# Last layer of a four-layer kernel: router and row numbers in another place of the order, maxima split at other points, expert tiles in slots 4 to 13

## The chip, the cores and the metric

The kernel is one program on one core of one Trainium2 chip. The metric is the device time of a launch in microseconds (us). Five engines run their own instruction streams side by side and meet at semaphores: TensorE (PE in the profile), VectorE (DVE), ScalarE (ACT), GpSimd (POOL) and SyncE (SP), which here only issues transfers. PEld is TensorE loading weights.

## The reference, cut to what matters

Four layers in a row work on `x` of 4 x 1024 x 128. Only the last one is touched. It normalizes `x` and adds a causal attention of 16 heads (8 wide) and a mixture of 8 experts of which each row takes the best two:

```python
    qkv = (x @ W_qkv + b_qkv).reshape(b, s, h, 3 * hd)
    logits = jnp.einsum('bshd,bkhd->bhsk', q, k) / np.sqrt(hd)
    logits = jnp.where(mask[None, None, :, :], -jnp.inf, logits)
    attn = jax.nn.softmax(logits, axis=-1)
    out = jnp.einsum('bhsk,bkhd->bshd', attn, v).reshape(b, s, d)
    return out @ W_out + b_out
...
    router_logits = x_flat @ router_w.T
    router_probs = jax.nn.softmax(router_logits, axis=-1)
    top_k_probs, top_k_idx = jax.lax.top_k(router_probs, TOP_K)
    top_k_probs = top_k_probs / (top_k_probs.sum(axis=-1, keepdims=True) + 1e-08)
    cw = (jax.nn.one_hot(top_k_idx, E, dtype=x.dtype) * top_k_probs[..., None]).sum(axis=1)
    for e in range(E):
        h = new_gelu(x_flat @ w1[e].T + b1[e])
        out_e = h @ w2[e].T + b2[e]
        output = output + cw[:, e:e + 1] * out_e
...
    x = x + _L3_attn_ref(xn, ...) + _L3_ffn_ref(xn, ...)
```

## The kernel before

The last layer is one stage, `attn3_stage`, in which attention and experts are interleaved by hand. Attention is cut into 16 combinations `c` of a batch and a group of four heads. The stage runs over 19 **slots** of 48 **places**; tables of places (`SCORES_AT`, `SUMS_AT` and so on) say at which place of a slot every engine does which piece. All engines walk the same loops, so the tables set the order on each.

Slot `s` works on three things at a time:

- Scores of combination `s` (slots 0 to 15): PE `score` (L2794, with the causal constants at L2799), 20 units, each read by DVE `largest` (L3221), which keeps row maxima. At the slot's end DVE reduces them (L3331).
- Maxima of `s - 1`: PE turns them (`turn_max`, key "Z", L2807), DVE copies them (`turned_max`, L3228), POOL splits them into three bfloat16 parts (`split_max`, five instructions, L3365 to L3369), SP writes them beside the queries (`maxima`, L2680, six DMAs).
- The transposed scores of `s - 2` (`scoreT`, L2822): PE can't begin them before these DMAs have landed. ACT takes the exponential (L3013), POOL zeroes the masked half of the diagonal blocks (`causal`, L3375; for combinations 0, 14 and 15 PE does this at L2829), PE multiplies with the values (`sums`, L2848).

The experts: DVE `route` (L3164 to L3177) makes from the router's product the two best experts of each row and their shares; PE `count` (L2773, L2774) sums the one-hot rows; DVE `slots` (L3184 to L3206) turns the counts into a slot number for each of 2 x 4096 rows, sorted by expert. POOL scatters the rows by 64 indirect DMAs of 128 rows (L3389) to `expert_rows`. They are processed as 39 tiles of 256 rows, each with its own expert's weights: SP `load_tile` (five DMAs, L2691 to L2697; it waits until all scatters have landed), PE turns the rows (L2865), multiplies up (L2875) and down (L2885), ACT does the gelu between (L3023), DVE copies, SP stores. At the end POOL gathers the results back by 64 indirect DMAs (L3380) and DVE adds them, scaled, to `x` (`combine`, 16 instructions a batch, L3285). Slots 1, 5 and 9 also project the next batch (`project`), slots 6, 10, 14 and the end add the attention's output to `x`.

Three tables matter here. `FIRST_SLOT, LAST_SLOT` spread the 39 tiles evenly over slots 3 to 13, which gives 3, 4, 3, 4, 3, 4, 3, 4, 3, 4, 4. `SPREAD` and `SCATTER` say after which score unit (slots 0 and 1) and which group of four places (slot 2) POOL issues scatters. `SPLIT_AT` says before which group POOL does the split: 8 up to slot 15, 2 in slot 16. POOL runs its stream in order, so a scatter ahead of a split holds it up. Only two PSUM bank pairs serve the scores, the maxima, the row transposes and the down products; they are handed out in turn (`s_at`, `take_s`), and each taker waits for the reader of the last but one.

Of the kernel before, what the change touches and what calls it, by code (L numbers as in the profile page):

```python
# [23 lines left out]
B, S, D = 4, 1024, 128  # L24
# [3 lines left out]
NCH = TOK // CH  # L28
# [2256 lines left out]
def layer2(k, L):  # L2285
    with ExitStack() as ctx:
# [10 lines left out]
NI = B * NG  # L2297
# [25 lines left out]
PARTS_AT = (4, 13, 16, 19, 22, 40, 42)  # L2323
MAX_AT, SPLIT_AT = (2, 20), (8, 2)
SUMS_AT = (7, 13, 16, 19, 22, 29, 30, 34, 40, 47, 47), \
# [5 lines left out]
OUT_AT = (42, 41), (32, 37)  # L2331
FIRST_SLOT, LAST_SLOT = 3, 13
PROJECT = {1: 1, 5: 2, 9: 3}
PER_SLOT = {s: range((s - FIRST_SLOT) * NTILE // (LAST_SLOT + 1 - FIRST_SLOT),
                     (s + 1 - FIRST_SLOT) * NTILE // (LAST_SLOT + 1 - FIRST_SLOT))
            for s in range(FIRST_SLOT, LAST_SLOT + 1)}
GATHER = {14: (0,), 15: (1,), 16: (2,), 17: (3,)}
SPREAD = ((0, 0, 0, 1, 1, 1, 1, 1, 1, 1, 1, 1, 1, 1, 2, 2, 2, 2, 2, 2), (1, 1, 1, 1, 1, 1, 1, 1, 1, 1, 1, 1, 1, 1, 1, 1, 2, 2, 2, 2))
SCATTER = (3, 3, 3, 3, 3, 2, 0, 0, 0, 0, 0, 0)
ON_PE = (0, NI - 2, NI - 1)  # L2340
# [78 lines left out]


def max_turned(s, place):
    return 0 <= s - 1 < NI and place == MAX_AT[s >= NI]
# [27 lines left out]
def ring_tables():  # L2450
# [7 lines left out]
    def add(table, key):  # L2458
        table[key] = len(table)

    def project(b, part):
        if part < 2:
            for t in range(2):
                add(t_at, ("P", b, part, t))
        elif part == 2:
            add(s_at, ("V", b))
# [5 lines left out]
    for i in range(2, NCH):  # L2472
        add(t_at, ("N", i))
    project(0, 2)
    add(s_at, ("G",))
    for s in range(SLOTS + 1):
        b = s - 2
        for place in range(PLACES):
# [18 lines left out]
            for bb, u in by_batch(s, place, OUT_AT):  # L2497
                add(s_at, ("Y", bb, u))
            if s == 0 and place == 3:
                add(s_at, ("C",))  # L2500
            for bb, part in projected(s, place):
# [4 lines left out]
def attn3_stage(k, R):  # L2506
# [15 lines left out]
    with ExitStack() as ctx:  # L2522
# [99 lines left out]
        with nc.Block() as block:  # L2622
# [121 lines left out]
            def _(pe):  # L2744
# [24 lines left out]
                def count():  # L2769
                    bank = take_s("C")  # L2770
                    when(pe, VR, "cw1")
                    all_hot = hot.rearrange("p r t e -> p (r t e)")
                    pe.matmul(k.ps[:, bank, :], k.triu[:], all_hot, start=True, stop=True)  # L2773
                    pe.matmul(k.ps[:, bank + 1, :], k.ones[:], all_hot, start=True, stop=True).then_inc(s_done, 1)  # L2774
# [153 lines left out]
                for i in range(3, NCH):  # L2928
                    turn_normed(i)
                    route(i - 1)  # L2930
                project(0, 2)
                route(NCH - 1)
                pe.wait_ge(ready, 9)
                pe.wait_ge(o_zero, 1)
                for s in range(SLOTS + 1):
                    b = s - 2
                    for place in range(PLACES):
# [19 lines left out]
                        for x, u in by_batch(s, place, OUT_AT):  # L2957
                            out_project(x, u)
                        if s == 0 and place == 3:
                            count()  # L2960
                        for x, part in projected(s, place):
# [121 lines left out]
            def _(dve):  # L3083
# [212 lines left out]
                rest_low(0)  # L3296
                normalize(7)
                values(0)
                route()
                dve.wait_ge(mx_zero, 1)  # L3300
                for s in range(SLOTS + 1):
                    first = s
                    for place in range(PLACES):
# [10 lines left out]
                        for x, u in by_batch(s, place, MERGE_AT):  # L3314
                            out_turned(x, u)
                        for x, u in by_batch(s, place, OUT_AT):
                            residual(x, u)
                        if s == 0 and place == 3:
                            slots()
                        for x, part in projected(s, place):  # L3320
# [12 lines left out]
                    for n in GATHER.get(s - 1, ()):  # L3333
                        combine(n)

            @block.gpsimd
            def _(pool):
# [56 lines left out]
                for s in range(SLOTS):  # L3394
# [6 lines left out]
                    if s >= 2:  # L3401
                        pool.wait_ge(parts, min(s - 1, NI))
                        for g in range(GROUPS):
                            if g == SPLIT_AT[s >= NI] and s - 1 < NI:
                                split_max(s - 1)
                                pool.wait_ge(parts, s)
# [148 lines left out]
```

## Time and profile before

| what | value |
|---|---|
| median of 3 runs | 2204.67 us (2203.06 to 2205.88) |
| the profiled execution | 2206.71 us, of which the trace's span is 2204.9 us |
| PE busy in the span | 1872.5 us (85%) |
| DVE, ACT, POOL busy | 1787.8, 1380.7, 1296.8 us |
| the last layer's slots in the span | from about 1509 us to the end |

A page of the profile gives each engine's busy time; an answer of the trace gives instructions in order of time, with the idle time before them and who ended it, or the busy time of each engine in stretches. The stretches used below are the slots as PE runs them. "x16" behind an instruction is a run of 16 alike, merged; the time then is that of the run.

### The profile page before, as it was taken

How to read it: one execution, taken by the hardware profiler on the slowest of the kernel's cores; microseconds unless marked ns; L12 is line 12 of the kernel's file. 1: busy time of each engine (PE TensorE's matmuls, PEld its weight loads, DVE VectorE, ACT ScalarE, POOL GpSimd, SP SyncE). 2: the span in 40 equal slices, each digit the busy share in tenths (PEclk: the TensorE clock that was granted, in tenths of full speed). 3: DMA queues.
4: the chain of work that ended last, by engine and by line, in shares of the span. 5: the costliest groups of instructions: out<-in, count | busy, mean ns of one | idle time of the engine just before them, and what ended most of it. 6: DMA issues, size and time to landing. Idle time of an engine off the chain costs nothing. (4 is left out here: it accounts for less than half of the span.)

```text
span 2204.9 us, 32675 instructions
## 1 busy us (share of the span) xinstructions
PE 1872.5 (85%) x10276; PEld 996.0 (45%) x10276; DVE 1787.8 (81%) x2181; ACT 1380.7 (63%) x2604; POOL 1296.8 (59%) x954
## 2 busy tenths in 40 slices
PE   5898989888989897777988499985759999999986
PEld 5333333333333333333565288863325455455532
DVE  6699999999999999977878899987847667667783
ACT  3676666666666666456335577761347777777766
POOL 4799999999998999932226255552741111111276
PEclk7999999999999999899998699995679999999998
DMA  3355444555444455540102000002333333333212
GB/s 79 112 160 149 151 156 157 154 156 166 143 151 149 153 155 155 159 134 0 31 12 81 1 0 0 0 19 77 85 98 94 103 112 94 103 113 94 76 38 75
DMA packets 156309, 217.53 MB, mean 99 GB/s; under 512 B 31722, under 2 KB 68602, under 8 KB 155546
## 3 DMA queue, kind: packets, MB, share of 16 engines
q1 hardware_dynamic: 152074, 207.41, 31.1%
q0 software_dynamic: 4096, 8.40, 1.5%
q8 instruction: 72, 1.18, 0.2%
q14 instruction: 67, 0.55, 0.1%
HBM read 196.59 MB, written 23.86 MB: 100 GB/s over the span
## 5 line engine op out<-in xcount | busy, mean ns | idle before, releaser
L1035 POOL TENSOR_TENSOR m_dBx<-m_du,m_rowB 128x1024 f32<-128x1024 f32 x256 | 605.0, 2391 | 4.4 <-DMA m_rowB<-bc_rows 4.2
L758 PE MATMUL ps<-m_hC,ident 128*128 128x512 f32 x1024 | 513.3, 648 | 99.1 <-DVE m_hC L1117 99.0
L3221 DVE TENSOR_REDUCE a_mx<-ps 128x2 f32<-128x1024 f32 (+2 forms) x320 | 345.0, 1114 | 113.5 <-PE ps L2794 55.6
L934 ACT ACTIVATE ps<-m_delta,m_A 128x512 f32<-128x512 f32 x512 | 332.7, 682 | 143.4 <-DVE m_hC L1117 112.7
L3013 ACT ACTIVATE a_pT<-ps 128x512 f32<-128x512 f32 (+2 forms) x640 | 317.9, 561 | 155.4 <-PE ps L2822 137.1
L758 PEld LDWEIGHTS ps<-m_hC,ident 128*128 128x128 f32 x1024 | 203.7, 207 | 391.9 <-issue 232.0
L3375 POOL TENSOR_SCALAR_AFFINE_SELECT a_pT<-a_pT 128x512 f32<-128x512 f32 x104 | 66.1, 637 | 390.1 <-ACT a_pT L3013 388.6
L1117 DVE TENSOR_TENSOR m_hC<-ps,m_rowC 128x1024 f32<-128x1024 f32 x176 | 215.4, 1224 | 16.7 <-issue 1.3
L1108 DVE TENSOR_TENSOR_SCAN ps<-ps,m_dBx 128x1024 f32<-128x1024 f32 x88 | 201.1, 2285 | 33.2 <-ACT ps L934 21.2
L1045 POOL TENSOR_TENSOR m_hC<-m_h,m_rowC 128x1024 f32<-128x1024 f32 x80 | 194.5, 2432 | 46.0 <-DVE m_h L1108 45.8
L1108 DVE TENSOR_TENSOR_SCAN ps<-ps,m_carry,m_dBx 128x1024 f32<-128x1024 f32 x88 | 206.3, 2345 | 5.5 <-ACT m_dBx L959 4.6
L2848 PE MATMUL ps<-a_pT,l_v 128*9 128x512 f32 (+3 forms) x1536 | 161.1, 500 | 2.3 <-POOL a_pT L3375 1.9
L2794 PE MATMUL ps<-a_k,a_q 48*128 48x512 bf16 (+3 forms) x768 | 132.8, 352 | 28.4 <-DVE a_mx L3221 18.1
L2822 PE MATMUL ps<-a_q,a_k 51*128 51x512 bf16 (+3 forms) x768 | 123.0, 339 | 31.9 <-ACT a_pT L3013 16.9
L713 PE MATMUL ps<-pad,e_conv_w 128*128 128x512 f32 x256 | 116.6, 599 | 1.2 <-DVE m_diag L1069 1.2
L2822 PEld LDWEIGHTS ps<-a_q,a_k 51*128 51x128 bf16 x768 | 36.3, 95 | 133.4 <-ACT a_pT L3013 92.6
L1108 DVE TENSOR_TENSOR_SCAN m_h<-ps,m_carry,m_dBx 128x1024 f32<-128x1024 f32 x40 | 93.6, 2341 | 0.0
L1108 DVE TENSOR_TENSOR_SCAN m_h<-ps,m_dBx 128x1024 f32<-128x1024 f32 x40 | 91.3, 2282 | 1.5 <-POOL m_dBx L1035 0.6
L3389 POOL DMA_INDIRECT expert_rows<-l_xn,l_slot x64 | 61.7, 964 | 48.1 <-DVE a_mx L3221 31.9
L2146 POOL TENSOR_TENSOR c_xw<-c_x,l_wb 128x256 f32<-128x256 f32 x32 | 19.6, 613 | 102.4 <-ACT c_x L2193 102.4
L2794 PEld LDWEIGHTS ps<-a_k,a_q 48*128 48x128 bf16 x768 | 39.0, 97 | 90.2 <-DVE a_mx L3221 59.1
L2885 PE MATMUL ps<-a_w,a_h 128*128 128x128 f32 x624 | 78.4, 280 | 0.0
(410 smaller groups left out, 3601.5 us busy)
## 6 DMA issues: line engine op xcount, KB each, us to landing
m_rowB<-bc_rows SPq DMA_DIRECT2D x256, 256.0 KB, 4.0
m_rowC<-bc_rows SPq DMA_DIRECT2D x256, 256.0 KB, 3.5
a_w<-in_L3f_w1T SPq DMA_DIRECT2D x39, 256.0 KB, 2.6
a_w<-in_L3f_w2T SPq DMA_DIRECT2D x39, 256.0 KB, 3.8
expert_rows<-in_zero_rows SPq DMA_DIRECT2D x39, 128.0 KB, 2.6
a_xs<-expert_rows SPq DMA_DIRECT2D x39, 128.0 KB, 2.3
expert_out<-a_y SPq DMA_DIRECT2D x39, 128.0 KB, 3.6
qk_parts<-a_part SPq DMA_DIRECT2D x18, 256.0 KB
```

The source lines that it names most:

```text
L713: mm = pe.matmul(o, wk[:, d, tap, c * P:c * P + P], pad[:, b * ROW + shift:b * ROW + shift + CH], start=tap == 0, stop=tap == CONV - 1)
L758: mm = pe.matmul(ps[:, bankY + c, :], k.ident[:], hC[:, n % NBUF, c, :], start=False, stop=n % NS == NS - 1)
L934: act.activation(decays(n)[:, c, :], delta[:, i % 2, c, chunk(i, x)], ACT.Exp, scale=An[:, ITEMS[i][0], c, s:s + 1]).then_inc(decayed, 1)
L1035: pool.tensor_tensor(dBx[:, n % NBUF], du[:, i % 2, :, chunk(i, x)], rowB[:, n % 4, :].unsqueeze(1).to_broadcast([P, HALF, CH]), ALU.mult) ...
L1045: pool.tensor_tensor(hC[:, n % NBUF], states(n), rowC[:, n % 4, :].unsqueeze(1).to_broadcast([P, HALF, CH]), ALU.mult).then_inc(hc_pool, 1)
L1108: dve.tensor_tensor_scan(time(states(n)), time(decays(n)), time(dBx[:, n % NBUF]), carry[:, s, f:f + 1] if x else 0.0, ALU.mult, ALU.add). ...
L1117: dve.tensor_tensor(hC[:, n % NBUF], states(n), rowC[:, n % 4, :].unsqueeze(1).to_broadcast([P, HALF, CH]), ALU.mult).then_inc(hc_dve, 1)
L2794: mm = pe.matmul(k.ps[:, bank + r, j * w:j * w + w], qs[u][rows, e, t * P:t * P + P], ks[u][rows, e, x:x + w], start=True, stop=not diag, ...
L2822: mm = pe.matmul(k.ps[:, tbank(n + r), j * w:j * w + w], ks[u][rows, e, kt * P:kt * P + P], qs[u][rows, e, q0:q0 + w], start=True, stop=no ...
L2848: mm = pe.matmul(k.ps[32 * hd:32 * hd + HD + 1, bankO, CH - w:CH], R["v"][:, c, kt, hd, :], pT[:, g % 3, hd, 0:w], start=kt == 0, stop=kt ...
L3013: act.activation(dst, src, ACT.Exp).then_inc(t_read, 1)
L3221: dve.tensor_reduce(mx[:, c % 2, :, es[0]:es[0] + len(es), t, x // CH], src, AX_X, ALU.max)\
```

## The change

- The router's last product is issued ahead of the values' product on PE (`project(0, 2)`), and DVE's `route` ahead of `values(0)`. `count` and `slots` leave place 3 of slot 0 and stand ahead of slot 0. `count` waits for the last step of the top-two search ("r_hot2") and no more for the shares.
- The scatters are dealt out anew (the sum is 64 in both): 20 and 30 in slots 0 and 1 instead of 23 and 24, 14 instead of 17 in slot 2. The split of slot 2 stands at group 0, ahead of that slot's scatters.
- The first tile slot is 4 instead of 3: the 39 tiles now lie as 3, then nine times 4.
- At the end: combination 15's maxima are turned at place 2 of slot 16 instead of 20, and split at group 0 instead of 2; the gathers of batches 2 and 3 are both issued in slot 16; the last `combine` stands between the last `out_turned` and the last `residual`, instead of behind it.

```diff
-MAX_AT, SPLIT_AT = (2, 20), (8, 2)
+MAX_AT, SPLIT_AT = (2, 2), (8, 0)
-FIRST_SLOT, LAST_SLOT = 3, 13
+FIRST_SLOT, LAST_SLOT = 4, 13
-GATHER = {14: (0,), 15: (1,), 16: (2,), 17: (3,)}
+GATHER = {14: (0,), 15: (1,), 16: (2, 3)}
...
+def split_at(s):
+    return MAX_AT[0] // 4 if s == 2 else SPLIT_AT[s >= NI]
...
-                    when(pe, VR, "cw1")
+                    when(pe, VR, top2_names("r")[-1])
...
+                route(NCH - 1)
                 project(0, 2)
-                route(NCH - 1)
+                count()
...
-                        if s == 0 and place == 3:
-                            count()
...
+                route()
                 values(0)
-                route()
+                slots()
...
                             out_turned(x, u)
+                            if (x, u) == (B - 1, 1):
+                                combine(x)
...
-                        if s == 0 and place == 3:
-                            slots()
...
                     for n in GATHER.get(s - 1, ()):
-                        combine(n)
+                        if n < B - 1:
+                            combine(n)
...
-                            if g == SPLIT_AT[s >= NI] and s - 1 < NI:
+                            if g == split_at(s) and s - 1 < NI:
```

What this does on PE at the layer's front. Before (L2764 router, L2756 values, L2794 and L2799 first scores, L2773 and L2774 `count`):

```order
L2764 MATMUL ps<-l_router,xnT 128x8 x4
L2756 MATMUL ps<-l_wqkv,xnT 128x128 x8
L2764 MATMUL ps<-l_router,xnT 128x8 x4
L2794 MATMUL ps<-a_k,a_q 128x128 x2
L2799 MATMUL ps<-a_consts_bf 128x128 x4
L2794 MATMUL ps<-a_k,a_q 128x128 x2
L2799 MATMUL ps<-a_consts_bf 128x128 x4
L2773 MATMUL ps<-a_h,triu 128x512
L2774 MATMUL ps<-a_h,ones 128x512
```

And now (the same lines stand five further down in the file):

```order
L2769 MATMUL ps<-l_router,xnT 128x8 x8
L2761 MATMUL ps<-l_wqkv,xnT 128x128 x8
L2778 MATMUL ps<-a_h,triu 128x512
L2779 MATMUL ps<-a_h,ones 128x512
L2799 MATMUL ps<-a_k,a_q 128x128 x2
L2804 MATMUL ps<-a_consts_bf 128x128 x4
```

The router's last four products moved ahead of the values, and the first score unit behind `count`.

On POOL, from the first scatter to the first masks, before (each run of L3365 to L3369 is a split):

```order
L3389 DMA expert_rows<-l_xn,l_slot 9984x128 x24
L3365 CAST a_m_parts<-a_mT 32x128
L3366 TENSOR_TENSOR a_mr<-a_mT,a_m_parts 32x128
L3367 CAST a_m_parts<-a_mr 32x128
L3368 TENSOR_TENSOR a_mr<-a_mr,a_m_parts 32x128
L3369 CAST a_m_parts<-a_mr 32x128
L3389 DMA expert_rows<-l_xn,l_slot 9984x128 x40
L3365 CAST a_m_parts<-a_mT 32x128
```

And now, where L3371 to L3375 is the split and L3395 the scatter:

```order
L3395 DMA expert_rows<-l_xn,l_slot 9984x128 x21
L3371 CAST a_m_parts<-a_mT 32x128
L3372 TENSOR_TENSOR a_mr<-a_mT,a_m_parts 32x128
L3373 CAST a_m_parts<-a_mr 32x128
L3374 TENSOR_TENSOR a_mr<-a_mr,a_m_parts 32x128
L3375 CAST a_m_parts<-a_mr 32x128
L3395 DMA expert_rows<-l_xn,l_slot 9984x128 x29
L3371 CAST a_m_parts<-a_mT 32x128
```

The second split has 50 scatters ahead of it instead of 64; the other 14 stand behind it, ahead of the first mask.

On DVE at the program's end (L3262 `out_turned`, L3270 `residual`, L3285 `combine`), before:

```order
L3241 TENSOR_TENSOR a_att<-ps,a_rs 128x4x32
L3262 COPY a_aT<-ps 128x512
L3270 TENSOR_TENSOR x_tm<-x_tm,ps 128x512
L3285 SCALAR_TENSOR_TENSOR x_tm<-a_h,l_cwr,x_tm 128x128 x16
```

And now, the same three at L3266, L3289 and L3274:

```order
L3245 TENSOR_TENSOR a_att<-ps,a_rs 128x4x32
L3266 COPY a_aT<-ps 128x512
L3289 SCALAR_TENSOR_TENSOR x_tm<-a_h,l_cwr,x_tm 128x128 x16
L3274 TENSOR_TENSOR x_tm<-x_tm,ps 128x512
```

The last `combine` moved ahead of the last `residual`.

## Rows read from the trace of the kernel before

**Rows 1.** Slots 3, 11, 12, 13, 15: length; busy PE, PEld, DVE, ACT, POOL; clock, DMA, GB/s

```profile
1627.00:1674.50 47.50, 38.43 (x343) 19.79 (x343) 25.18 (x31) 28.13 (x56) 6.53 (x13) 0.82 0.42 123
...
1968.70:2004.50 35.80, 35.30 (x351) 18.75 (x343) 25.69 (x33) 27.92 (x56) 6.67 (x14) 1.00 0.33 93
2004.50:2043.90 39.40, 39.00 (x377) 22.28 (x369) 26.59 (x35) 29.58 (x60) 6.76 (x14) 1.00 0.34 96
2043.90:2083.20 39.30, 38.89 (x377) 22.28 (x369) 26.49 (x35) 29.58 (x60) 6.66 (x14) 1.00 0.22 65
...
2112.70:2141.20 28.50, 24.02 (x270) 8.40 (x267) 24.88 (x32) 20.73 (x42) 21.47 (x28) 1.00 0.15 38
```

**Rows 2.** DVE in order of time: start us, us, instruction, count [idle before <-releaser]

```profile
1507.69 1.68 DVE L3150 TENSOR_TENSOR l_v<-ps,l_bias_v 128x128 f32<-128x128 f32 x8 [10.66 <-PE ps L2756]
1509.28 0.41 DVE L3164 COPY a_h<-ps 128x256 f32<-128x256 f32 x1
...
1517.15 0.42 DVE L1160 TENSOR_TENSOR a_h<-l_iota,a_h 128x256 f32<-128x256 f32 x1
...
1522.79 0.69 DVE L3184 COPY a_h<-ps 128x512 f32<-128x512 f32 x1 [3.21 <-PE ps L2774]
...
1531.56 20.48 DVE L3221 TENSOR_REDUCE a_mx<-ps 128x4 f32<-128x1024 f32 x19
```

**Rows 3.** PE in order of time, at the layer's front

```profile
1504.25 3.40 PE L2756 MATMUL ps<-l_wqkv,xnT 128*128 128x128 f32 x16
1507.49 0.96 PE L2764 MATMUL ps<-l_router,xnT 128*128 128x8 f32 x8
...
1519.00 2.04 PE L2773 MATMUL ps<-a_h,triu 128*128 128x512 f32 x2 [8.97 <-DVE l_cwr L3177]
```

**Rows 4.** POOL in order of time, slots 0 to 2

```profile
1535.48 1.23 POOL L3389 DMA_INDIRECT expert_rows<-l_xn,l_slot  x1 [29.03 <-DVE a_mx L3221]
...
1566.15 1.45 POOL L3366 TENSOR_TENSOR a_mr<-a_mT,a_m_parts 32x128 f32<-32x128 f32 x1
...
1619.18 0.95 POOL L3389 DMA_INDIRECT expert_rows<-l_xn,l_slot  x1 [0.30 <-issue]
...
1621.84 0.28 POOL L3369 CAST a_m_parts<-a_mr 32x128 bf16<-32x128 f32 x1
```

**Rows 5.** SP's issues in order of time, between slots 2 and 3

```profile
1622.14 3.73 SPq L2680 DMA_DIRECT2D a_q<-a_m_parts  x6
1627.03 0.41 SPq L2691 DMA_DIRECT2D a_xs<-expert_rows  x1
```

**Rows 6.** PE at the start of slot 3, in order of time

```profile
1627.08 0.61 PE L2822 MATMUL ps<-a_q,a_k 51*128 51x512 bf16 x2 [12.70 <-DMA a_q<-a_m_parts]
...
1632.91 0.66 PE L2865 MATMUL ps<-ident,a_xs 128*128 128x128 f32 x2 [4.04 <-DMA a_w<-in_L3f_w2T]
...
1639.46 0.66 PE L2865 MATMUL ps<-ident,a_xs 128*128 128x128 f32 x2 [2.53 <-DMA a_w<-in_L3f_w2T]
```

**Rows 7.** Line L2865, PE's idle time ahead of it: releaser, us, times

```profile
  DMA a_w<-in_L3f_w2T: 8.4, 3
```

**Rows 8.** DVE in order of time, slots 15 to 18

```profile
2112.96 0.22 DVE L3331 TENSOR_REDUCE a_m<-a_mx 128x32 f32<-128x64 f32 x1
...
2139.62 5.42 DVE L3285 SCALAR_TENSOR_TENSOR x_tm<-l_xn,l_cwr,x_tm 128x128 f32<-128x128 f32 x16
...
2196.90 4.29 DVE L3285 SCALAR_TENSOR_TENSOR x_tm<-a_h,l_cwr,x_tm 128x128 f32<-128x128 f32 x16 [4.88 <-DMA a_h<-expert_out,l_slot]
```

**Rows 9.** POOL in order of time, slots 16 to 18

```profile
2151.84 0.28 POOL L3365 CAST a_m_parts<-a_mT 32x128 bf16<-32x128 f32 x1 [4.33 <-issue]
...
2154.23 0.98 POOL L3380 DMA_INDIRECT a_h<-expert_out,l_slot  x1 [0.41 <-POOL a_m_parts L3369]
...
2161.96 2.59 POOL L3380 DMA_INDIRECT a_h<-expert_out,l_slot  x1 [0.30 <-ACT a_pT L3013]
...
2194.29 0.96 POOL L3380 DMA_INDIRECT a_h<-expert_out,l_slot  x1 [0.30 <-issue]
```

More of the change, by code:

```diff
@@ L2336 @@
             for s in range(FIRST_SLOT, LAST_SLOT + 1)}
-GATHER = {14: (0,), 15: (1,), 16: (2,), 17: (3,)}
-SPREAD = ((0, 0, 0, 1, 1, 1, 1, 1, 1, 1, 1, 1, 1, 1, 2, 2, 2, 2, 2, 2), (1, 1, 1, 1, 1, 1, 1, 1, 1, 1, 1, 1, 1, 1, 1, 1, 2, 2, 2, 2))
-SCATTER = (3, 3, 3, 3, 3, 2, 0, 0, 0, 0, 0, 0)
+GATHER = {14: (0,), 15: (1,), 16: (2, 3)}
+SPREAD = ((1,) * 20, (1, 2) * 10)
+SCATTER = (4, 4, 4, 2, 0, 0, 0, 0, 0, 0, 0, 0)
 ON_PE = (0, NI - 2, NI - 1)
@@ L2473, in ring_tables @@
         add(t_at, ("N", i))
+    add(s_at, ("G",))
     project(0, 2)
-    add(s_at, ("G",))
+    add(s_at, ("C",))
     for s in range(SLOTS + 1):
@@ L2498, in ring_tables @@
                 add(s_at, ("Y", bb, u))
-            if s == 0 and place == 3:
-                add(s_at, ("C",))
             for bb, part in projected(s, place):
@@ L3315, in _ @@
                             out_turned(x, u)
+                            if (x, u) == (B - 1, 1):
+                                combine(x)
                         for x, u in by_batch(s, place, OUT_AT):
                             residual(x, u)
-                        if s == 0 and place == 3:
-                            slots()
                         for x, part in projected(s, place):
```

## The prediction, made before the changed kernel was run

> **What bounds the kernel now.** I read the last layer first, since nothing else is touched, and there the busy time by stretch, one stretch a slot as PE runs it. In the middle of the layer PE is the bound: slot 11 with three tiles lasts 35.8 us, of which PE is busy 35.30, slots 12 and 13 with four tiles 39.4 and 39.3, of which 39.00 and 38.89, at the full clock [rows 1]. So there PE's work costs what it takes, and waits elsewhere cost nothing. Three places are not like that; the reader should look there for who is late.
>
> Ahead of slot 3 PE does nothing for 12.70 us and is then released by the DMA of the maxima [rows 6]. SP issued it from 1622.14 us on, right behind the split that ended at 1622.12, and that split began the moment the last scatter was done, at 1620.13 [rows 4, 5]. So the bound is POOL's queue of 64 scatters, begun at 1535.48, each 0.95 us of work and 0.30 of idle time, 1.26 together [rows 4].
>
> Slot 3 itself lasts 47.5 us, though it has three tiles like the slot of 35.8. PE waits three times for a tile's weights, 8.4 us in all, because the loads were issued only at 1627.03, behind maxima and scatters, and the granted clock is 0.82 of full [rows 1, 5 to 7].
>
> At the end DVE adds batch 3's results from 2196.90 on, after 4.88 us of waiting for the last gather. POOL issued that one at 2194.29: its gathers went on only at 2154.23, behind a split for which it had waited 4.33 us, since PE turns those maxima at place 20 [rows 8, 9].
>
> **The front, 4.5 us.** DVE's `route` starts at 1509.28; the top-two search ends at 1517.57, 8.29 into it, and the last share releases PE's `count` at 1519.00 [rows 2, 3]. `route` had waited for the router's last product, which stood behind the values' 3.4 us on PE [rows 3]. Now that product is done at 1504.25 + 0.9 = 1505.15, so `route` starts at about 1505.3, the search ends at 1513.6 and the shares at 1514.9. `count` starts at 1513.6 and takes what it took before, 1519.00 to 1522.75; so `slots` starts at 1517.4 instead of 1522.79. `values` (1.68) fits between, 1514.9 to 1516.6. `slots` takes 1531.56 - 1522.79 = 8.77 [rows 2] and ends at 1526.2. One score unit (0.69) that had been read ahead of it comes behind it now, with 0.2 for a bank pair that is free late: 1526.2 + 0.9 + 20.5 = 1547.6 against 1552.0 [rows 2], 4.5 us earlier. Slot 0 is DVE's to bound, slot 1 by and large too, so I carry the 4.5 on to slot 2. Bounds: 3.0, if the shift meets PE at its low clock in another way, and 5.4, the whole shift of `slots`.
>
> **POOL's wait, 12.7 us.** Scatters can start when the first score unit has been read, 1526.9, and 1 us after it, 1527.9. Then come 21 of them (26.5 us), a split, 29 more (36.6) and the second split. That one took 2.0, from 1620.13 to 1622.12; the first took longer, since one of its steps took 1.45 where the later ones take 0.4 [rows 4]; I give it 2 to 4. So the second is done at 1595.0 to 1597.0. SP takes 3.73 for the maxima, and PE had them 1.2 later [rows 5, 6]: 1600 to 1602. PE wants them 4.5 us earlier than the 1614.4 at which it ran dry, at 1609.9. The wait is gone with 8 us to spare. What is late next on POOL: 14 scatters (17.7 us) stand behind that split, to 1613 to 1615, and the first mask of slot 3 wants POOL at about 1613. I put 0 for it, since there are three buffers of exponentials, and 1 in the range.
>
> **Slot 3 without tiles, 20.5 us.** The nearest row is slot 15, no tiles and no projection: 28.5 us by the stretch, with masks between gathers on POOL, and 2139.62 - 2112.96 = 26.7 us from the end of one slot's maxima on DVE to the end of the next [rows 1, 8]. I take 27.0, since slot 3 has no gathers; bounds 26.5 and 30. 47.5 - 27.0 = 20.5 saved, of which 8.4 are waits for weights and most of the rest work that goes elsewhere.
>
> Will those waits come back at slot 4? SP issues the four loads behind `maxima(2)`. POOL splits these right after slot 3's fourth mask, since groups 4 to 7 make it wait for nothing: I put that 10 us into the slot and its end at 12 (an estimate from slot 15's order). Then 3.7 for the maxima, 1.2 to the first load, 5.9 from first load to first use, and (1639.46 - 1632.91) / 2 = 3.3 for each further tile [rows 5, 6]: 23, 26 and 29 us. The first three are wanted at 27, 29 and 29. So I put 0, and up to 8.4 in the range.
>
> **The tiles moved, -10.5 us.** Of 39 tiles three leave slot 3 and one slot 4; slots 5, 7, 9 and 11 take them. So three more lie in slots where PE is the bound. The fourth tile's price is 39.3 - 35.8 = 3.5 us; the mean of the first three, (35.8 - 27) / 3 = 2.9, is the lower bound [rows 1]. The upper one is 4.5, since slots 5 and 9 also project and I can't part their cost. 3 x 3.5 = 10.5.
>
> **The end, 3.5 us.** Combination 15's maxima are turned at place 2; DVE copies them once `combine(0)` is done, at 2139.62 + 5.42 = 2145.04 [rows 8]. The split runs 2145.5 to 2147.5, and 32 gathers follow from 2147.9, where 30 began at 2154.23. One at 2161.96 took 2.59 us, 1.63 more than its neighbours, and I count two such [rows 9]. The last is issued at 2147.9 + 31 x 1.26 + 2 x 1.63 = 2190.2, 4.0 earlier. It lands 2.6 later, as before, so the last `combine` (4.29) runs 2192.8 to 2197.1; the residual behind it ends at 2197.9. The last write was at 2196.90 + 4.29 = 2201.19 [rows 8]. That is 3.3, and one of the two stores that follow goes out earlier: 3.5. Bounds: 0, if the maxima's copy is late, and 5.
>
> Those held-up gathers, both in the midst of a `combine` on DVE: the row shows 2.59 where the last one shows 0.96 [rows 9]. The Trainium skill, "SBUF — State Buffer", section "Who interferes with whom", says that a VectorE instruction with two SBUF inputs contends with a GpSimd instruction that reads SBUF, and whichever comes second is blocked; by that rule, the trace agrees. If it did not hold here, the last gather would be issued 3.3 us earlier still and the end would give 6.8 instead of 3.5.
>
> **Sum.** 4.5 + 12.7 + 20.5 - 10.5 + 3.5 = 30.7 us less. Against the profiled execution, 2206.71 us (span 2204.9 and 1.8 around it), 2176.0. The median of the runs, 2204.67, stands 2.0 below the profiled one: 2174.0. All terms at their best give 5.4 + 12.7 + 21.0 - 8.7 + 5 = 35.4, which is 2169; all at their worst 3.0 + 11.7 + 17.5 - 13.5 + 0 - 8.4 = 10.3, which is 2194.
>
> **Rivals.** *The weights are late again.* The loads land in slot 4 as they did in slot 3, and PE waits up to 8.4 us. For it: the third tile is due just when it is wanted, by an estimate of POOL's place. Against: the first has 4 us. It gives 30.7 - 8.4 = 22.3 less, 2182. Chance 0.12.
>
> *POOL stays the bound.* If scatters are held up as the gather at 2161.96 was, by DVE's `slots`, by the subtractions of slot 1's projection or by reads in SBUF, the second split comes later. It decides from 8 us of delay on, that is from five such hold-ups; with ten, 16 us, PE waits 8 again and the change gives 22 less, 2183. Against: in the old order 64 scatters kept their pace beside the same maxima. Chance 0.07.
>
> *The wait moves to the masks.* The 14 scatters behind the second split hold up slot 3's first mask. At 1615 instead of 1613 it is nothing; with the hold-ups of the last rival, 5 to 8 us later, all of it is lost in slot 3: 23 to 26 less, 2179 to 2182. Then the change wouldn't do what it says. Chance 0.08.
>
> *Four tiles a slot cost more than PE's share.* In nine slots in a row SP has four loads and four stores ahead of the stacks of slot `s + 2`, and two bank pairs serve four tiles beside the scores. If that cost 3.4 us a slot on top, nine times, the 30.7 would be gone; beyond it the kernel is slower than before, 2207 with 3.7. Against it: slots 12 and 13 had four tiles one behind the other, at 39.4 and 39.3 with PE busy all but 0.4 [rows 1]. Chance 0.03.
>
> **How the numbers follow.** The rest, 0.70, is the forecast, 2174, with 2168 to 2180 as its own range. The next three rivals reach to 2183 or so, some of their cases beyond 2186. So 2168 to 2186 leaves out 0.15 to 0.2. Faster by over 0.2% (4.4 us, about what a measurement of this kernel can tell from no change) takes in all but the last rival and the worst sums: 0.96; within it 0.02; slower 0.02.
>
> **What would show it right or wrong.** In the changed kernel's trace: `slots` starting at 1517.4; the second split at about 1593 to 1595 behind 50 scatters, and PE not waiting for a maxima DMA at slot 3; a slot 3 of 27 us at the full clock; no wait of the first row transposes for weights; slots 7 and 11 at 39.3 us; in the last slot the last `combine` waiting for a gather that is issued 4 us sooner after slot 16's start than before. A slot 4 over 40 us, a gap at slot 3's first masks, or slots 5 and 9 longer by much more than 3.5 would make it wrong at that term.

## The result, and the profile after

The changed kernel takes 2173.18 us (median of 4 runs, 2171.57 to 2177.9); the kernel before 2205.28 in the same comparison. The ratio is 0.9864, with a 95% interval of 0.9843 to 0.9885: 1.4% faster. In a second set of runs it was 2173.24 us, ratio 0.9862 (0.9846 to 0.9879). 2174.0 had been forecast. The profiled execution took 2173.8 us, its span is 2172.0.

Runs of the same kernel differ by several us. Most of that lies ahead of the last layer, where nothing was changed, so I measure inside the layer, from anchors on DVE: the end of its last normalization (L3118 before, L3122 after) is the layer's start, and the start of the reduce that closes each combination's maxima (L3331, now L3336) ends a slot. Before, the layer took 707.87 us from its start to the span's end; now 677.06, which is 30.81 less, where 30.7 was forecast. All stretches below lie between these anchors, so "slot 3" is from slot 2's reduce to slot 3's.

| stretch | before | after | less | forecast |
|---|---|---|---|---|
| slots 0 to 2 | 117.46 | 112.90 | 4.56 | 4.5 |
| slot 3 | 60.42 | 28.79 | 31.63 | 33.2 (12.7 + 20.5) |
| slots 4 to 15 | 464.57 | 474.67 | -10.10 | -10.5 |
| behind slot 15 | 65.42 | 60.70 | 4.72 | 3.5 |

The busy time by stretch of the changed kernel, for slots 0, 3, 4, 5, 7 and behind slot 15. The columns are start and end, length, busy PE, PEld, DVE, ACT, POOL with counts, PE's granted clock, DMA share, GB/s:

```profile
1494.94:1546.19 51.25, 31.12 (x184) 18.97 (x184) 38.92 (x69) 3.90 (x7) 24.20 (x20) 0.57 0.28 90
...
1607.84:1636.63 28.79, 24.98 (x267) 8.94 (x265) 22.93 (x26) 20.77 (x42) 9.88 (x17) 0.94 0.40 119
1636.63:1672.46 35.83, 35.32 (x345) 18.76 (x343) 25.67 (x33) 27.92 (x56) 6.69 (x13) 1.00 0.33 97
1672.46:1720.43 47.97, 44.78 (x393) 25.50 (x389) 32.73 (x47) 37.50 (x69) 6.05 (x12) 1.00 0.31 88
...
1764.86:1804.15 39.29, 38.89 (x371) 22.28 (x369) 26.52 (x35) 29.58 (x60) 6.69 (x13) 1.00 0.33 92
...
2111.30:2172.00 60.70, 43.32 (x477) 16.95 (x477) 23.93 (x80) 39.38 (x85) 38.27 (x41) 0.89 0.28 74
```

And of the kernel before, slot 3, slot 5 and the end:

```profile
1614.49:1674.91 60.42, 38.84 (x345) 19.91 (x347) 25.77 (x33) 28.13 (x56) 12.81 (x23) 0.77 0.35 104
...
1714.24:1758.41 44.17, 41.11 (x367) 21.92 (x363) 31.99 (x44) 35.62 (x65) 6.05 (x12) 1.00 0.35 101
...
2139.48:2204.90 65.42, 45.08 (x477) 18.03 (x477) 24.03 (x80) 39.62 (x85) 39.20 (x41) 0.83 0.26 69
```

In slot 3 PE was idle for 60.42 - 38.84 = 21.6 us and is now idle for 3.8. The later slots have PE busy almost throughout, as the prediction read them from [rows 1].

**The front**, against [rows 2, 3]. DVE and PE of the kernel after, in order of time:

```profile
1504.06 0.42 DVE L3168 COPY a_h<-ps 128x256 f32<-128x256 f32 x1 [9.12 <-PE ps L2769]
...
1511.94 0.42 DVE L1160 TENSOR_TENSOR a_h<-l_iota,a_h 128x256 f32<-128x256 f32 x1
...
1516.30 0.69 DVE L3188 COPY a_h<-ps 128x512 f32<-128x512 f32 x1 [0.95 <-PE ps L2779]
```

```profile
1500.60 3.42 PE L2769 MATMUL ps<-l_router,xnT 128*128 128x8 f32 x16
1503.87 3.56 PE L2761 MATMUL ps<-l_wqkv,xnT 128*128 128x128 f32 x16
1512.51 2.05 PE L2778 MATMUL ps<-a_h,triu 128*128 128x512 f32 x2 [5.08 <-DVE a_h L1160]
```

The layer starts 2.09 us earlier in this execution (1494.94 against 1497.03), so "in before's time" below means a time of this trace plus 2.09. `slots` starts 21.36 us after that start, where it was 1522.79 - 1497.03 = 25.76: 4.40 earlier. PE's `count` (L2778) now waits for the search's last step and no more for the shares, as forecast.

**POOL**, against [rows 4]: the first scatter, the second split, its last step, the last scatter, and the first masks.

```profile
1526.69 1.23 POOL L3395 DMA_INDIRECT expert_rows<-l_xn,l_slot  x1 [22.33 <-DVE a_mx L3225]
...
1592.12 0.30 POOL L3371 CAST a_m_parts<-a_mT 32x128 bf16<-32x128 f32 x1
...
1593.83 0.28 POOL L3375 CAST a_m_parts<-a_mr 32x128 bf16<-32x128 f32 x1
...
1611.01 0.96 POOL L3395 DMA_INDIRECT expert_rows<-l_xn,l_slot  x1 [0.30 <-ACT a_pT L3017]
1611.98 1.23 POOL L3381 TENSOR_SCALAR_AFFINE_SELECT a_pT<-a_pT 128x512 f32<-128x512 f32 x2
```

The split is done at 1594.1 us, 13.7 ahead of slot 3, and PE's 12.70 us of waiting for the maxima [rows 6] have no successor. What it does wait for in slot 3 is the first mask, which POOL can write only behind the last scatter:

```profile
1612.78 1.83 PE L2853 MATMUL ps<-a_pT,l_v 128*9 128x512 f32 x8 [1.15 <-POOL a_pT L3381]
...
1622.40 1.05 PE L2853 MATMUL ps<-a_pT,l_v 128*9 128x512 f32 x8
```

The second row is the same product at the full clock: for a while after the wait PE ran at the low one. SP issued the loads of slot 4's tiles from 1624.69 us on, and PE waited for none of them; [rows 7] has no counterpart.

**The end**, against [rows 8, 9]: POOL's first, two long and last gather, and DVE's last `combine`.

```profile
2119.64 0.98 POOL L3386 DMA_INDIRECT a_h<-expert_out,l_slot  x1 [0.41 <-POOL a_m_parts L3375]
...
2132.39 2.85 POOL L3386 DMA_INDIRECT a_h<-expert_out,l_slot  x1 [0.30 <-issue]
...
2155.71 1.54 POOL L3386 DMA_INDIRECT a_h<-expert_out,l_slot  x1 [0.30 <-issue]
...
2161.33 0.95 POOL L3386 DMA_INDIRECT a_h<-expert_out,l_slot  x1 [0.30 <-issue]
```

```profile
2164.00 4.29 DVE L3289 SCALAR_TENSOR_TENSOR x_tm<-a_h,l_cwr,x_tm 128x128 f32<-128x128 f32 x16 [3.83 <-DMA a_h<-expert_out,l_slot]
```

### The profile page after: what moved, and what is told of

It is laid out like the page before. It is cut to its first block and busy times, and to the rows that moved or that the text cites. A ratio compares the mean times of both kernels' runs of the same rounds, so it can differ in the third digit from the quotient of the medians.

```text
span 2172.0 us, 32672 instructions
## 1 busy us (share of the span) xinstructions
PE 1866.3 (86%) x10276; PEld 993.4 (46%) x10276; DVE 1787.1 (82%) x2181; ACT 1378.2 (63%) x2602; POOL 1295.0 (60%) x954
## 5 line engine op out<-in xcount | busy, mean ns | idle before, releaser
L2799 PE MATMUL ps<-a_k,a_q 48*128 48x512 bf16 (+3 forms) x768 | 132.1, 351 | 27.5 <-DVE a_mx L3225 18.0
L3395 POOL DMA_INDIRECT expert_rows<-l_xn,l_slot x64 | 62.1, 971 | 41.5 <-DVE a_mx L3225 24.8
L2799 PEld LDWEIGHTS ps<-a_k,a_q 48*128 48x128 bf16 x768 | 38.8, 97 | 89.8 <-DVE a_mx L3225 60.3
L713 PEld LDWEIGHTS ps<-pad,e_conv_w 128*128 128x128 f32 x256 | 49.0, 192 | 63.8 <-issue 61.2
```

The lines of the kernel that those rows point to most:

```text
L713: mm = pe.matmul(o, wk[:, d, tap, c * P:c * P + P], pad[:, b * ROW + shift:b * ROW + shift + CH], start=tap == 0, stop=tap == CONV - 1)
L2799: mm = pe.matmul(k.ps[:, bank + r, j * w:j * w + w], qs[u][rows, e, t * P:t * P + P], ks[u][rows, e, x:x + w], start=True, stop=not diag, ...
```

## Experiments: each part alone, on the kernel before

**The front alone.**

```diff
-    project(0, 2)
     add(s_at, ("G",))
+    project(0, 2)
+    add(s_at, ("C",))
...
-                    when(pe, VR, "cw1")
+                    when(pe, VR, top2_names("r")[-1])
...
+                route()
                 values(0)
-                route()
+                slots()
```

> The kernel before with the new front alone: router and row numbers ahead of slot 0. The theory of the prediction: the scatters start some 4.6 us earlier because the fourth score unit is read so much earlier, and the whole chain of POOL up to slot 3 moves with them, so 4 to 5 us less in all, with PE still waiting 12 to 13 us for the maxima ahead of slot 3. Rival: POOL's chain has slack that the trace doesn't show, or the shift is lost at PE's low clock in slot 1; then 0 to 2 us less.

Measured: 2197.27 us, ratio 0.9979 (0.9962 to 0.9996). Slots 0 to 2 took 113.26 us, 4.2 less; slot 3 60.36 as before. PE waits as long as before at slot 3:

```profile
1622.84 0.61 PE L2821 MATMUL ps<-a_q,a_k 51*128 51x512 bf16 x2 [12.90 <-DMA a_q<-a_m_parts]
```

So the front moves everything by some 4 us, POOL's queue with it, and shortens no wait behind it.

**The split alone.**

```diff
-                            if g == SPLIT_AT[s >= NI] and s - 1 < NI:
+                            if g == (0 if s == 2 else SPLIT_AT[s >= NI]) and s - 1 < NI:
```

> The kernel before with one change: the split of slot 2 ahead of that slot's scatters, tiles still from slot 3. The theory: PE no longer waits for the maxima, but the first row transposes of slot 3 still wait for weights whose loads wait for the last scatter, which ends as late as before (1622); so the wait of 12.7 us turns into one for the weights, and only 2 to 4 us of the 12.7 are gained. Rival: the waits are independent terms, as a sum of rows would have it, and 12 us are gained.

Measured: 2198.44 us, ratio 0.9985 (0.9969 to 1.0001). Slot 3 took 59.24 us, 1.2 less, which is below the 2 to 4 that were expected, and far from the rival's 12; the interval of the whole time takes in no change at all. The wait for the maxima is gone, and another stands in its place, longer:

```profile
1633.38 0.66 PE L2865 MATMUL ps<-ident,a_xs 128*128 128x128 f32 x2 [16.44 <-DMA a_w<-in_L3f_w2T]
```

The loads of tiles wait for all scatters, wherever the split stands, and slot 3 wants its tiles at once.

**The tiles alone.**

```diff
-FIRST_SLOT, LAST_SLOT = 3, 13
+FIRST_SLOT, LAST_SLOT = 4, 13
```

> The kernel before with one change: the first tile slot is 4, the split where it was. The theory: the 12.7 us for the maxima stay, slot 3 loses its three tiles and the 8.4 us of waiting for weights, and the other slots take 10 more; 9 to 11 us less in all. Together with b2_split this is less than the 21.5 that both give in the changed kernel, since each alone leaves the other's wait. Rival: terms add, and this alone gives what is left of the 21.5 after b2_split's 12, 9 or so; the two runs together tell them apart by their sum, 12 to 14 against 21.

Measured: 2193.1 us, ratio 0.9961 (0.9945 to 0.9978). Slot 3 took 42.99 us, 17.4 less, and slots 4 to 11 10.1 more, 340.1 against 330.0. The wait for the maxima stays:

```profile
1628.94 0.61 PE L2822 MATMUL ps<-a_q,a_k 51*128 51x512 bf16 x2 [14.21 <-DMA a_q<-a_m_parts]
```

**The end alone.**

```diff
-MAX_AT, SPLIT_AT = (2, 20), (8, 2)
+MAX_AT, SPLIT_AT = (2, 2), (8, 0)
-GATHER = {14: (0,), 15: (1,), 16: (2,), 17: (3,)}
+GATHER = {14: (0,), 15: (1,), 16: (2, 3)}
...
+                            if (x, u) == (B - 1, 1):
+                                combine(x)
```

> The kernel before with the end alone changed: combination 15's maxima turned at place 2 and split at group 0 of slot 16, all 32 last gathers in slot 16, the last combine ahead of the last residual. Theory: the last gather is issued 4 to 5 us earlier and the end moves with it, 3.5 to 5 us less. Rival: the attention's own chain (last transposes, output projection) is right behind, and 2 or less is gained.

Measured: 2201.27 us, ratio 0.9987 (0.9971 to 1.0004), which the whole time can't tell from no change. The end took 61.30 us against 65.42. But that isn't all due to the change. Of the five executions with the old end it took 65.42, 65.28, 63.94, 63.19 and 63.11 us, at a granted clock of 0.83, 0.83, 0.89, 0.90 and 0.90: the same instructions. Their mean is 64.2. The eight with the new end and with `combine` in its places took 59.75 to 62.14, mean 61.0. The clock comes in through POOL's split of combination 15. With the old end PE turns these maxima at place 20, and the split was done 14.3 us after slot 15 in the two slowest executions, where PE's clock was low right behind that slot, and 12.3 in the two fastest, where it was not. With the new end it was done at 7.9 to 8.0 in all eight, though the clock fell there in two of them too. So the new end is worth 3.2 us on these means and 2.1 against the two fastest alone. Why the clock fell there in some executions and not in others wasn't tried.

## Experiments: the parts together

The split and the tiles took 1.2 + 17.4 = 18.6 us off slot 3 one by one, the whole change 31.6. So both were put on the kernel before.

**Split and tiles.** The two edits above.

> The kernel before with two parts of the change and no more: the split of slot 2 at group 0, and the first tile slot 4 instead of 3. Alone, the split took 1.2 us off slot 3 and the tiles 17.4 us, together 18.6, while the whole change took 31.6 off it. Theory (two waits in a row, of which each alone hides the other: without the split's move PE waits for the maxima whatever the tiles do, without the tiles' move it waits for their weights as soon as the maxima come): both together take about 30 us off slot 3, 60.4 to some 30, and with 10 us given back in the later slots the layer is about 20 us shorter, a time near 2185. Rival (the parts add up, and the front is what makes the rest): slot 3 at about 42 us and the layer 9 us shorter, 2196. I also expect PE to wait 1 to 5 us for the first mask of slot 3, since the scatters behind the split start 4.5 us later against PE's clock... of the old front, with 17 of them instead of 14.

Measured: 2183.66 us, ratio 0.9903 (0.9879 to 0.9926). Slot 3 took 34.70 us, 25.7 less, and the layer 687.74, 20.1 less. So the theory of two waits in a row holds: 25.7 is more than 18.6, and PE waits for neither maxima nor weights. Slot 3 is 4.7 us longer than the 30 that were expected, because the wait for the mask, expected at 1 to 5 us, is longer than that:

```profile
1627.42 1.89 PE L2848 MATMUL ps<-a_pT,l_v 128*9 128x512 f32 x8 [6.35 <-POOL a_pT L3375]
```

POOL's last scatters and the masks right behind them, in the same kernel:

```profile
1624.39 0.96 POOL L3389 DMA_INDIRECT expert_rows<-l_xn,l_slot  x1 [0.30 <-issue]
1625.65 0.95 POOL L3389 DMA_INDIRECT expert_rows<-l_xn,l_slot  x1 [0.30 <-issue]
1626.62 1.24 POOL L3375 TENSOR_SCALAR_AFFINE_SELECT a_pT<-a_pT 128x512 f32<-128x512 f32 x2
```

Rival 3 of the prediction, the wait that moves to the masks, is what happens when these two parts are made alone, and in the changed kernel 1.15 us of it is left.

**The changed kernel with the old front.** The first diff above, the other way round; scatters, tiles and end stay as changed.

> The changed kernel with the old order at the layer's front alone (values ahead of the router's last product, first score unit and place 3 ahead of count and slots). Forecast's theory: slots 0 to 2 are 4.5 us longer, nothing else moves, 4.5 us more in the layer. Rival: the front's shift is taken up behind, by POOL's scatters and the first mask of slot 3: then the 4.5 us come back in part in slot 3 and the layer is 0 to 2 us longer, or it is 6 to 7 us longer if the mask is later still.

Measured: 2174.32 us, ratio 0.9871 (0.9847 to 0.9895), and a layer of 677.91 us, 0.85 longer than with the new front. Slots 0 to 2 are 3.8 longer, but slot 3 took 26.39 instead of 28.79, at the full clock and without a wait for a mask. The rival was right: part of what the front gains is given back in slot 3. But not all of it. Of slot 3's 2.4 us, 1.4 are low clock that a second execution of the changed kernel didn't have (below), and the rest of the way to 0.85 is play: slots 6 and 10, whose clock differs, were 1.8 shorter with the old front, and the end, whose gathers were held up for longer, 1.2 longer. With these three stretches left out, the new front is worth 1.4 us, and 2.3 against that second execution. POOL's first scatters of this kernel show why it isn't 3.8:

```profile
1528.29 1.23 POOL L3398 DMA_INDIRECT expert_rows<-l_xn,l_slot  x1 [24.88 <-DVE a_h L3208]
1530.42 0.96 POOL L3398 DMA_INDIRECT expert_rows<-l_xn,l_slot  x1 [0.90 <-DVE a_mx L3227]
```

In the old front the first score unit is read ahead of the row numbers, so the first scatter starts as soon as these are there, 34.3 us after the layer's start. In the new one it stands behind the first unit, at 31.75. So the front brings PE 3.8 us, but the first scatter only 2.55, and POOL's 64 scatters end 2.7 us sooner: at 1613.71 - 1493.99 = 119.7 us after the layer's start with the old front, 117.0 with the new. In between the old front loses 0.60 us, as the second scatter waits 0.90 instead of 0.30 for its unit, and the new one 0.44, in a scatter that took 1.40 us beside a subtraction of DVE. Against the kernel with split and tiles this one has the new deal of the scatters (20, 30, 14) too: there the queue ended at 1626.60 - 1500.56 = 126.0. The new deal alone brings the queue's end 6.3 us forward (4.5 of it at the first scatter, which no longer waits for the fourth score unit), and with it the mask. That is the part that the kernel with split and tiles lacks.

One rule then holds for all seven executions in which slot 3 can be held up by its first mask alone. Taken from slot 3's start, the queue ended and PE waited for the first mask:

| kernel | queue's end | wait | slot 3 |
|---|---|---|---|
| split and tiles | 9.3 | 6.35 | 34.70 |
| changed kernel | 4.1 | 1.15 | 28.79 |
| changed kernel, again | 4.0 | 1.02 | 27.38 |
| with the additions behind (below) | 4.0 | 1.02 | 27.39 |
| with the old front | 3.0 | none | 26.39 |
| first scatter ahead (below), twice | 2.7 | none | 26.34, 26.35 |

The wait is what the queue's end exceeds 3.0 us by.

**The changed kernel with slot 2's split behind all scatters.**

```diff
-    return MAX_AT[0] // 4 if s == 2 else SPLIT_AT[s >= NI]
+    return SPLIT_AT[s >= NI]
```

> The changed kernel with slot 2's split behind all of the 64 scatters, at group 8 as before. Forecast's theory: 14 more scatters at 1.26 us each stand ahead of the split, which ends at about 1611.7 instead of 1594.1, so that the maxima land at about 1616.6 where PE wants them at 1607.7: PE waits about 9 us at slot 3, its clock falls, and the layer is 9 to 11 us longer. Rival (the split's place is worth little, as it was alone in the old order): 0 to 2 us longer.

Measured: 2184.54 us, ratio 0.9914 (0.9887 to 0.9941). Slot 3 took 37.28 us, 8.5 more; the layer is 8.5 longer, just under the 9 to 11 expected. The wait is the one expected:

```profile
1620.68 0.61 PE L2827 MATMUL ps<-a_q,a_k 51*128 51x512 bf16 x2 [8.95 <-DMA a_q<-a_m_parts]
```

Alone the split's place was worth 1.2 us, here 8.5: it depends on what is late behind it.

**Three scatters behind slot 3's masks.**

```diff
-SCATTER = (4, 4, 4, 2, 0, 0, 0, 0, 0, 0, 0, 0)
+SCATTER = (4, 4, 3, 0, 0, 0, 0, 0, 0, 0, 0, 0)
...
+                            if s == 3 and g == 4:
+                                scatter(3)
```

> The changed kernel with the last three of the 14 scatters moved out of slot 2, behind the four first masks of slot 3 (before its group 4). Theory (the scatters behind the second split hold up the first mask, PE then waits 1.15 us and runs at the low clock to 1616): the first mask is written 3.8 us earlier, PE's wait and the low clock go, slot 3 lasts about 27.0 instead of 28.8 us, and the layer is 1.2 to 2 us shorter. Rival (PE would have been slow there in any case, or the three scatters hold up the split of slot 3 and with it the weights of the first tiles): no change, or 1 to 4 us longer by waits for weights in slot 4.

Measured: 2181.05 us, ratio 0.9898 (0.9879 to 0.9917). Both sides were right about their slot. Slot 3 took 26.35 us, 2.4 less, and slot 4 took 40.41, 4.6 more, since the weights are late now; the layer is 2.6 longer. SP's issues of slot 4's third tile, and PE:

```profile
1634.18 2.08 SPq L2700 DMA_DIRECT2D a_b<-in_L3f_b  x1
1636.36 0.38 SPq L2702 DMA_DIRECT2D a_w<-in_L3f_w2T  x1
```

```profile
1640.06 0.41 PE L2870 MATMUL ps<-ident,a_xs 128*128 128x128 f32 x2 [3.29 <-DMA a_w<-in_L3f_w2T]
```

The three scatters put off the split of slot 3, whose last step ends at 1621.5 instead of 1619.8, and the loads behind it by 1.6 us. In the changed kernel the same load was issued at 1632.95, ahead of an issue of 1.90 us on SP; here one of 2.08 us fell in front of it, and 1.6 became 3.4. And PE, no longer held by the mask, wanted it 2.1 us sooner: slot 4 starts at 1634.56 instead of 1636.63. Together the load came 5.5 us later for PE, which waited 3.29 of them, so the margin on this tile's weights was 2.2 us. The prediction's first rival is that close.

**The first scatter ahead.** The lesson of the two last: begin the queue sooner, and move nothing behind it.

```diff
-SPREAD = ((1,) * 20, (1, 2) * 10)
+SPREAD = ((0,) + (1,) * 19, (1, 2) * 10)
...
                 when(pool, VS, "int")
+                scatter(1)
                 for s in range(SLOTS):
```

> The changed kernel with POOL's first scatter ahead of the wait for slot 0's first score unit; the other 19 of slot 0 follow as they did. In the changed kernel the row numbers are done at 1525.08 us, yet the first scatter waits for a score unit read behind them and starts at 1526.69. Theory (the 64 scatters at 1.26 us each are one queue, the front's 4.5 us reached it only in part, and so its end came too late for slot 3's first mask): the whole queue moves 1.2 to 1.5 us ahead, the last scatter to about 1609.6, PE doesn't wait for the mask, slot 3 lasts 26.4 us as with the old front instead of 28.8, the loads of slot 4's tiles come 1.2 us earlier and don't hold up slot 4. 2.4 us less in the layer, a time near 2170.8. Rival (the mask is late by more than the 1.15 us that PE is seen waiting, or the low clock there doesn't hang on the wait): 0 to 1 us less.

Measured: 2175.76 us, ratio 0.9877 (0.9859 to 0.9894), while the layer is 673.28 us, 3.8 less than the changed kernel's: slot 3 took 26.34 us and slot 4 35.83. The whole time doesn't show it; this execution reached the last layer only at 1500.72. So both kernels were run once more, side by side.

> The changed kernel once more, beside the kernel with the first scatter ahead, on the same chip and in the same rounds. Slot 3 lasted 28.79 us in one execution and 27.39 in another whose order is the same up to there. I expect 27.4 to 28.8 us again with a wait of PE for the first mask, a layer of 676 to 679 us, and a time near 2174.

> The kernel with the first scatter ahead once more, beside the changed kernel. Theory: slot 3 again at 26.3 to 26.4 us without a wait for the mask, the layer 1 to 3.8 us shorter than the changed kernel's, and the time lower by as much, which five rounds may just tell apart. Rival: the layer's shortening of 3.78 us in one execution was mostly the run-to-run play of slots 6, 10 and the end, and the gain is 1 us or nothing.

Measured: 2173.24 us (2172.4 to 2177.99) and 2172.21 us (2169.42 to 2181.99); against before 0.9862 (0.9846 to 0.9879) and 0.9869 (0.9847 to 0.9892). The times don't tell the two apart. In the traces they entered the layer at 1493.82 and 1493.54, and it took 677.18 and 674.06 us: 3.1 less with the first scatter ahead. 1.0 of it is slot 3 (27.38 against 26.35) and is the wait for the mask. 1.3 is the end: its last gather was issued 1.3 us sooner after slot 15, since the long gathers took 2.04 and 2.59 us where they took 3.12 and 2.83. 1.2 is slot 10, at a clock of 1.00 against 0.96, and 0.4 goes back in slot 6. The order in slots 6 and 10 is the same, so what the edit itself brings for certain is the 1.0. Yet slot 10 ran at the full clock in both executions of this kernel and in none of the other twelve; whether that hangs on the edit isn't settled.

**The additions behind the last gather.**

```diff
                             if (x, u) == (B - 1, 1):
-                                combine(x)
+                                for n in range(1, B):
+                                    combine(n)
...
-                        if n < B - 1:
+                        if n < 1:
                             combine(n)
```

> The changed kernel with the sums of expert results of batches 1 and 2 moved behind the last gather, beside batch 3's, so that DVE adds nothing while POOL issues the last 32 gathers. Forecast's theory (two of these gathers are held up by the additions): no gather takes over 1.1 us, where two took 2.85 and 1.54; the last is issued 2.5 us sooner after the split than in the changed kernel. DVE then has 12.9 us of additions in a row, of which about 4 fall into its wait for the gather, so the end is 2 to 5 us longer. Rival (the hold-ups come from something else, such as the residual's write or the stores of batch 0's output): two gathers still take 1.5 to 2.9 us.

Measured: 2175.86 us, ratio 0.989 (0.9869 to 0.9912). From the first of the last 32 gathers to the last:

```profile
2118.84 0.98 POOL L3387 DMA_INDIRECT a_h<-expert_out,l_slot  x1 [0.41 <-POOL a_m_parts L3376]
...
2157.91 0.95 POOL L3387 DMA_INDIRECT a_h<-expert_out,l_slot  x1 [0.30 <-issue]
```

That is 39.07 us, 31 steps of 1.26, and none in between took over 1.0; in the changed kernel it was 2161.33 - 2119.64 = 41.69. So the two long gathers come from the additions beside them. The end took 63.92 us, 3.2 more, as DVE is now the last.

The traces also show for how long. The two runs of additions beside the long gathers of the changed kernel:

```profile
2130.12 4.28 DVE L3289 SCALAR_TENSOR_TENSOR x_tm<-l_xn,l_cwr,x_tm 128x128 f32<-128x128 f32 x16
...
2152.14 4.28 DVE L3289 SCALAR_TENSOR_TENSOR x_tm<-a_h,l_cwr,x_tm 128x128 f32<-128x128 f32 x16
```

The first run ends at 2134.40, and the gather of 2.85 us at 2132.39 + 2.85 = 2135.24; the second at 2156.42, and the gather of 1.54 us at 2157.25. Both end 0.83 us behind the last addition. The same holds in all 13 executions with such runs beside the gathers: each of the 26 runs holds up one gather for long, and that one ends 0.82 to 0.83 us behind the run. So a held-up gather isn't delayed by one addition of 0.27 us but by all that are left of the run, and the sooner it meets the run, the longer it takes: 3.12 us when it starts 2.0 into the run, 1.54 when it starts 3.57 into it.

## Why the prediction was right

The mechanisms hold, by the experiments above. That the layer's 30.81 us meet the forecast of 30.7 to 0.1 is luck: slot 3 gave 1.6 less than its terms, the end 1.2 more, the tiles took 0.4 less.

- **The front, 4.5 us: right in size, not in worth.** Slots 0 to 2 gave 4.56. `slots` began 1.0 us later than 1517.4 in before's time (1516.30 + 2.09 = 1518.4), mostly because `route` began at 1506.15 in that time and not at 1505.3. The step "I carry the 4.5 on" held for PE and not for POOL: I had the first scatter behind the first score unit in the working (1527.9 by that, 1528.8 measured in before's time) and didn't see that with the same deal of scatters the old front lets one run ahead of that unit. So POOL's queue gains 2.7 us from the front, and in the changed kernel the front is worth 1.4 to 2.3 us, not 4.5.
- **POOL's wait, 12.7 us: right.** It is gone, and the second split's end lies where it was expected: 1594.1, in before's time 1596.2, within 1595.0 to 1597.0.
- **The first mask, put at 0 with 1 in the range: short by 1.0 to 2.4 us.** The scatters' end was forecast for 1613 to 1615 and came at 1611.97 + 2.09 = 1614.1. POOL was wanted 3.0 us after slot 3's start, at 1612.9 in before's time, and "at about 1613" had been forecast. So both times were right, and the step from them to 0 was not: the three buffers of exponentials don't cover the difference. PE waited 1.02 to 1.15 us, and in one of three executions of this order the low clock added 1.4. Without it slot 3 takes 26.3 to 26.4, in the three kernels where the mask is in time.
- **Slot 3 without tiles, 27.0 us: right.** 27.38, 27.39 and 28.79 were measured, with the mask's wait in them, and 26.3 to 26.4 without it. That the terms 12.7 and 20.5 are both there only if both edits are made was not said: alone they gave 1.2 and 17.4, together 25.7.
- **No waits in slot 4: right.** 35.83 us, PE busy 35.32. The forecast had the third tile due just when it is wanted, at 29 us; its margin was 2.2. Three scatters in front of it brought 4.6 us back, so the first rival was close.
- **POOL stays the bound: it did not.** One scatter was held up, for 0.44 us, where 8 us would have been needed.
- **The tiles moved, 10.5 us: right.** Slots 7 and 11 cost 3.5 and 3.2 more, slot 4 3.5 less. Slots 5 and 9, whose cost couldn't be parted before, took 3.80 more each. PE's busy time rose there by 44.78 - 41.11 = 3.67, about as in slot 7; the other 0.13 is idle time. That makes 10.8 where 10.5 was counted; slots 6 and 10, whose clock differed, gave 0.8 back, which was in no term.
- **The end, 3.5 us: right in size.** The means over executions give 3.2, and the fastest with the old end 2.1; the 4.72 of the table contain a split that was late by PE's low clock in the execution before. The last gather is issued 2161.33 - 2111.30 = 50.0 us after slot 15's end, before 2194.29 - 2139.48 = 54.8: 4.8 earlier instead of 4.0, as the two hold-ups took 1.89 + 0.59 = 2.5 us where 3.3 was counted. In the second execution of the same kernel they took 3.12 and 2.83, 4.0 more than two plain ones. The forecast took 1.63 us for every hold-up, where the size hangs on how much of the run of additions is left. With the additions moved away there is no long gather in 32. The rule of the Trainium skill, "SBUF — State Buffer", section "Who interferes with whom" (a VectorE instruction with two SBUF inputs and a GpSimd instruction that reads SBUF contend, and the later one is blocked), had been weighed on one row; by this run, the trace agrees. That the hold-up lasts to the end of a whole run of 16 instructions, and not of one, is what the traces add.
- **The fourth rival,** tiles that cost more than PE's share in nine slots, fell: in slots 7, 8, 11, 12 and 13 PE is idle for 0.4 us, as in 39.29 - 38.89, and in slots 5 and 9 for 3.2, where it was idle for 3.1 with three tiles.

## What to carry to other kernels

When two waits stand in a row, taking away one alone can measure almost nothing: the split gave 1.2 us alone and 8.5 beside the other parts. Try the pair before dropping an edit, and price it by what is late behind both. Where one engine's in-order queue feeds several others, write down the queue's end against each of its users' due times: here the split, the mask and the weights all hung on the end of 64 scatters, and starting the queue one scatter sooner did what shifting scatters behind a user did not. For gains of 1 to 4 us in 2200, compare stretches between anchors and look at the clock beside them, since the total moves by more on its own.

## What the runs showed of the hardware

**The clock.** After the same wait the clock fell in some executions and not in others. PE waits 1.02 us for slot 3's first mask in the second execution of the changed kernel, and the product behind the wait runs at full speed, 1.05 us where the first execution has 1.83:

```profile
1612.06 1.05 PE L2853 MATMUL ps<-a_pT,l_v 128*9 128x512 f32 x8 [1.02 <-POOL a_pT L3381]
```

At the start of slot 10 PE waits for ACT. In the changed kernel the row transposes behind the wait take 1.27 us for four, and the slot's stretch shows a clock of 0.93:

```profile
1891.80 0.39 PE L2827 MATMUL ps<-a_q,a_k 51*128 51x512 bf16 x2 [2.80 <-ACT a_pT L3017]
...
1894.53 1.27 PE L2870 MATMUL ps<-ident,a_xs 128*128 128x128 f32 x4
```

With the first scatter ahead the same wait, to the hundredth, is followed by the same four in 0.83 us, at a clock of 1.00:

```profile
1889.96 0.39 PE L2827 MATMUL ps<-a_q,a_k 51*128 51x512 bf16 x2 [2.80 <-ACT a_pT L3017]
...
1892.14 0.83 PE L2870 MATMUL ps<-ident,a_xs 128*128 128x128 f32 x4
```

The two levels are 1.2 and 2.4 GHz, and slot 10's length follows the time at the low one: 46.28 us at a clock of 0.93, 44.7 to 44.8 at 0.96 and 43.57 at 1.00, over ten executions with the same four tiles. This wait of 2.80 us stands at the start of slot 6 and of slot 10 in all 14 executions, and the clock was low at it or right behind it in 26 of the 28 cases. The wait for the mask brought the low clock at 1.15 us and not at 1.02, in two other executions. So such a wait costs itself and 1.2 to 2.7 us more (1.4 at the mask), mostly at 2.8 us and now and then at 1.0 to 1.2. What decides it isn't settled: nothing in the order of these slots differs between the executions.

**Held-up gathers.** Beside a run of additions one gather takes 1.54 to 3.12 us, where a plain one takes 0.96, and it ends 0.83 us behind the run, as shown above. The others beside the same run took 0.95 to 1.13. Scatters beside DVE's two subtractions (1.22 us each, L3142) show the same: that of 1.40 us ends 0.83 behind the first subtraction, though the second has begun by then. Which gather of a run is the one held up isn't settled: in the 26 cases it started 0.16 to 0.19 us into an addition, but so did some that passed.
